# Graph attention and a mixture of experts on one core: where the normed row is added, which engines finish a tile, and the order of the opening loads

## Chip, cores, metric

One core of one Trainium2 chip runs the whole program in one launch. The metric is the device time of an execution in microseconds, the median of several runs of the same kernel.

## What is computed

There are 6250 nodes with 256 features and 206,250 edges, sorted by destination. Two layers follow each other. Shapes and names are cut to what matters:

```
h  = layernorm(x)                                  # (6250, 256)
z  = h @ W[head];  es = z.a_src;  ed = z.a_dst      # 4 heads of 64
e  = leaky_relu(es[src] + ed[dst], 0.01)
p  = exp(e - max over the edges of a destination)
x1 = x + (sum of p * z[src] over the edges) / (sum of p)

n      = layernorm(x1)                             # the "normed row"
logits = n @ gate_w + gate_b                       # 16 experts, the best 2 of each node
s0, s1 = softmax(top 2 logits)                     # s0 + s1 = 1
f_k    = relu(n @ w1[e_k] + b1[e_k]) @ w2[e_k] + b2[e_k]
y      = n + s0 * f_0 + s1 * f_1
out    = x1 + layernorm(y) * gamma + beta
```

Since s0 + s1 = 1, y is also s0 * (n + f_0) + s1 * (n + f_1).

## The kernel before, in words

The nodes lie in 49 tiles of 128 (`NT`; the last has 106 rows). The program has five stages, each ended by a barrier of all engines. Every engine has its own instruction stream. The helper `pipeline` (L50) writes such a stream out: for each round `i` it calls each listed function for item `i - lag`, in the order of the list, with a peeled head, a hardware loop and a tail. So the order within an engine is fixed by hand, and only semaphores tie the engines together.

- **Opening stage** (from L231). The SyncE queue (SP) loads `W`, then x in four parts of 12 tiles (`XC` = 4, `PART` = 12, L237), then the 106-row rest. It then waits for each part and passes the news on to VectorE (DVE) as `a_arrived` (L243), and after that stores the 49 projected tiles to `z_table` (L247). The ScalarE (ACT) queue loads the edge lists `src_raw` and `dst_raw` (L266 to L270) and gate_b, gamma and beta (L273). DVE forms the attention columns of `wcat` (L331, L332), the statistics of the first 12 tiles (L337), the inverse deviations (L171 to L176, L342), and then norms a tile (L355) for each that TensorE (PE) transposes (L456) and projects (L464). ACT copies both results from PSUM (L289, L297) into a ring of four `z_out`. GpSimd (POOL) sets `acc`, the sums of all tiles, to zero in one memset (L317).
- **Edge stage** (from L471). DVE first finds the largest and smallest source score; POOL takes the maximum over partitions (L541); from it comes `npass`, which every engine reads. Then 451 visits follow: POOL gathers rows of `z_table` by indirect DMA (L552), and PE, DVE and ACT weigh and sum them. This is the long stage, and the change leaves its loop alone.
- **Routing stage**. The new x1, its norm (kept in DRAM as `norm_rows`), the gate, and the lists of which node goes to which slot of which expert.
- **Expert stage** (L1093 on). Some 108 tiles of 128 slots. For a tile j, POOL fetches its normed rows by indirect DMA into `rows_sb` (`fetch`, L1140), PE transposes them (L1161), DVE copies the transpose (`copy_xT`, L1227), ACT copies `w1` (`copy_w1`, L1194) and then issues the load of the bias row `b2` of the expert, repeated on 128 partitions, into slot j mod 4 of `b2_sb` (L1198; the profile calls it `b_sb`). PE computes both products (L1171, L1183) with a relu on ACT between them (L1206). DVE adds the bias row (`add_b2`, L1232) and POOL stores the tile to `pair_rows` (`put`, L1147). Two orders matter for the change. On ACT, round j holds `copy_w1(j)`, the bias load of j and `relu(j-2)`; the load waits until `add_b2(j-4)` is done, as that frees the slot. On DVE, round i holds `copy_src(i)`, `copy_xT(i-3)`, `copy_dst(i-6)`, `add_b2(i-6)`.
- **Final stage** (L1242 on), 49 tiles, ring of 8. SP loads the two expert rows of each node and the normed row (L1316, L1317). ACT multiplies the first by s0 (L1262), POOL adds the normed row (L1270), DVE adds s1 times the second (L1279), takes the statistics (L1284, L1289), the inverse (L1293, the root is on ACT, L1257), subtracts the mean and multiplies by gamma (L1297), and multiplies by the inverse deviation and adds x1 + beta (L1303). SP stores the tile (L1324).

Of the kernel before, what the change touches and what calls it, by code (L numbers as in the profile page):

```python
# [33 lines left out]
RMAX = bass.bass_isa.ReduceOp.max  # L34
# [14 lines left out]
AHEAD = 6  # L49
ROWS = 4  # L50
# [41 lines left out]
def gnn_moe_kernel(nc, x, src, dst, W, a_src, a_dst, gate_w, gate_b, w1, b1, w2, b2, gamma, beta, out):  # L92
# [31 lines left out]
    def sem(name):  # L124
        return nc.alloc_semaphore(name=name)
# [10 lines left out]
    with whole:  # L136
# [27 lines left out]
        group_free = sb(graph, "group_free", [1, GROUPS], I32)  # L164

# [29 lines left out]
        a_x = [sem(f"a_x{i}") for i in range(XC + 1)]  # L195
        a_edges = sem("a_edges"); a_w = sem("a_w"); a_rows = sem("a_rows"); a_late = sem("a_late"); a_last = sem("a_last")
        a_vstep = sem("a_vstep"); a_bulk = sem("a_bulk"); a_arrived = sem("a_arrived"); 
        a_zeroed = sem("a_zeroed"); a_es = sem("a_es")
# [3 lines left out]
        a_xn = sem("a_xn"); a_xT_ps = sem("a_xT_ps"); a_xT = sem("a_xT"); a_z_ps = sem("a_z_ps")  # L202
        a_mod = sem("a_mod"); a_mod_saved = sem("a_mod_saved")
        a_z = sem("a_z"); a_store = [sem(f"a_store{i}") for i in range(4)]
        with ExitStack() as ctx:
# [13 lines left out]
            thr = sb(ctx, "thr", [P, 4])  # L219
            xn = sb(ctx, "xn", [P, 4, D])  # L220
            xnT = sb(ctx, "xnT", [P, 2, D])
            z_out = sb(ctx, "z_out", [P, 4, D + 2 * HEADS])
# [9 lines left out]
            def _(sp):  # L232
# [15 lines left out]
                pipeline(sp, NT, 4, 0, [(store, 0)])  # L248
                sp.wait_ge(a_mod, 1)
                sp.dma_start(dst_rows.rearrange("(b p f) -> p b f", p=P, f=P), dst_mod_h[:, :, :]).then_inc(a_mod_saved, 16)  # L250
                for s in range(4):
                    sp.wait_ge(a_store[s], 16 * len(range(s, NT, 4)))
# [3 lines left out]
            def _(act):  # L256
# [6 lines left out]
                act.wait_ge(a_padded, 3)  # L263
                tail = BLOCKS - 1
                for raw, e in ((src_raw, src), (dst_raw, dst)):
                    act.dma_start(raw[:, 0:tail, :], e[0:tail * P * P].rearrange("(b p f) -> p b f", p=P, f=P)).then_inc(a_edges, 16)  # L266
                    n = FULL_CHUNKS - tail * P
                    act.dma_start(raw[0:n, tail, :], e[tail * P * P:FULL_CHUNKS * P].rearrange("(p f) -> p f", f=P)).then_inc(a_edges, 16)
                    if E > FULL_CHUNKS * P:
                        act.dma_start(raw[n:n + 1, tail, 0:E - FULL_CHUNKS * P],  # L270
                                      e[FULL_CHUNKS * P:E].unsqueeze(0)).then_inc(a_edges, 16)
                for to, r in ((rows_bc[:, 2 * D:], gate_b), (affine[:, 0:D], gamma), (affine[:, D:2 * D], beta)):
                    act.dma_start(to, over(r.unsqueeze(0), [P, to.shape[-1]])).then_inc(a_late, 16)  # L273
# [17 lines left out]
                def copy_z(t, s, r):  # L291
                    act.wait_ge(a_z_ps, t + 1)
                    if not early(t, 4):
                        at, use = s % 4, r * (PART // 4) + s // 4
                        act.wait_ge(a_store[at], 16 * use)
                        act.wait_ge(a_es, t - 3)
                    nc.scalar.copy(z_out[:, s % 4, :], psZ[s % 2][:, 0:D + 2 * HEADS]).then_inc(a_z, 1)  # L297
                pipeline(act, NT, PART, PART, [(next_root, 0), (copy_xT, 0), (copy_z, 1)], tail=PART + 1)

            @block.gpsimd  # L300
            def _(pool):
# [11 lines left out]

                pool.wait_ge(a_edges, 16 * (6 if E > FULL_CHUNKS * P else 4))
# [1035 lines left out]
```

## Time and profile before

| | |
|---|---|
| median of 3 runs | 2931.32 us (2925.68 to 2935.93) |
| the profiled execution | 2933.89 us, of which the span of the trace is 2932.2 us |
| mean granted TensorE clock | 0.802 of full |
| busy: PE, DVE, ACT, POOL | 2224.2, 1807.8, 649.5, 1877.4 us |

How to read it: the profile gives for each engine the busy time, for each instruction its line, its start and duration, and for each stretch of idle time before one what ended it. PEld is the weight load of TensorE, which overlaps its products. A row with `ACTq` or `SPq` is a DMA issue on that queue; "to landing" counts from the start of the issue to the moment the transfer is seen. Line numbers in the rows are those of the kernel before; those of the changed kernel run up to 41 higher. A busy share of an engine is an average over five stages with different limits, so the stages are read one by one.

### The profile page before, as it was taken

To read this page: it belongs to the slowest core of one execution; us is meant where nothing else is said; L and a number is where in the kernel's file an instruction comes from. 1 tells how busy PE (TensorE), PEld (TensorE's weight loads), DVE (VectorE), ACT (ScalarE), POOL (GpSimd) and SP (SyncE) were. 2 spreads that over 40 slices of the span, in tenths; PEclk is the share of its full clock that TensorE was granted. 3 is DMA by queue.
4 is the path that set the end of the run, shared out by engine and by line. 5 is a ranking of instruction groups with operands and counts; after the bars stand their busy time and mean duration, and the time that the engine had idled before them with its cause. 6 is when DMAs were issued, how large, how long until landed. Compare 5 with 4: busy or idle time off the path is not lost. (4 is left out here: it accounts for less than half of the span.)

```text
span 2932.2 us, 63657 instructions
## 1 busy us (share of the span) xinstructions
PE 2224.2 (76%) x10753; PEld 1880.8 (64%) x10754; DVE 1807.8 (62%) x4852; ACT 649.5 (22%) x2612; POOL 1877.4 (64%) x1912
## 2 busy tenths in 40 slices
PE   3588778888778878778788788888855578999920
PEld 2477666676667766666666667667645358989920
DVE  6666666666666666666666666666668742222258
ACT  1311111111111111111111111111111234555532
POOL 2277777777777777777777777777753244545533
PEclk9877887877887778887887887787875589999965
DMA  4255555555555555555555555555541056333356
GB/s 147 88 142 137 135 134 136 135 135 135 135 134 135 136 133 136 138 135 134 135 136 135 134 135 137 134 134 135 137 134 63 25 189 186 104 100 106 104 165 206
DMA packets 298513, 386.43 MB, mean 132 GB/s; under 512 B 104451, under 2 KB 235883, under 8 KB 298475
## 3 DMA queue, kind: packets, MB, share of 16 engines
q0 software_dynamic: 87744, 243.02, 31.9%
q10 hardware_dynamic: 84912, 75.49, 10.5%
q1 hardware_dynamic: 125818, 67.52, 8.2%
q14 instruction: 28, 0.22, 0.0%
q8 instruction: 11, 0.18, 0.0%
HBM read 351.08 MB, written 33.93 MB: 131 GB/s over the span
## 5 line engine op out<-in xcount | busy, mean ns | idle before, releaser
L552 POOL DMA_INDIRECT ring<-z_table,idx_ring x1612 | 1552.1, 963 | 495.5 <-issue 452.2
L738 PE MATMUL psMb<-msg,xs 128*128 128x260 f32 x3608 | 1203.1, 491 | 259.9 <-DVE msg L649 258.2
L738 PEld LDWEIGHTS psMb<-msg,xs 128*128 128x128 f32 x3608 | 828.0, 241 | 433.8 <-issue 267.0
L727 PEld LDWEIGHTS psEb<-nodes,xs 128*128 128x128 f32 x3608 | 562.0, 227 | 260.2 <-issue 226.1
L727 PE MATMUL psEb<-nodes,xs 128*128 x3608 | 528.0, 274 | 156.6 <-DVE xs L607 153.8
L649 DVE TENSOR_TENSOR msg<-ring,psPb 128x1024 f32<-128x1024 f32 x451 | 545.7, 1210 | 0.0
L621 DVE TENSOR_TENSOR earg<-es_edge,psEb 128x16 f32<-128x16 f32 x451 | 76.5, 170 | 609.2 <-ACT es_edge L699 602.7
L699 ACT COPY es_edge<-ring 128x16 f32 x451 | 91.9, 204 | 1494.8 <-SPq L523 1321.9
L613 DVE TENSOR_TENSOR xs<-iota_f,psPb 128x512 f32<-128x512 f32 x451 | 306.2, 679 | 1.4 <-ACT psPb L708 0.2
L607 DVE TENSOR_SCALAR xs<-dst_bc,iota_p 128x512 f32<-128x512 bf16 x451 | 231.1, 513 | 39.9 <-issue 21.0
L1227 DVE COPY xT<-psXd 128x256 f32<-128x256 f32 x108 | 45.8, 424 | 317.6 <-PE psXd L1161 317.6
L1147 POOL DMA_INDIRECT pair_rows<-y_sb,dst_sb x108 | 107.6, 996 | 192.3 <-DVE src_sb L1216 124.2
L1171 PE MATMUL psHd<-xT,w_sb 128*128 128x128 f32 x1728 | 217.5, 281 | 0.0
L663 DVE TENSOR_TENSOR acc<-acc,psMb 128x260 f32 x451 | 188.6, 418 | 34.2 <-PE psMb L738 31.9
L1171 PEld LDWEIGHTS psHd<-xT,w_sb 128*128 128x128 f32 x1728 | 207.6, 197 | 0.6 <-issue 0.4
L1183 PE MATMUL psYd<-w_all,hid 128*128 x864 | 206.1, 382 | 0.0
L689 ACT ACTIVATE psPb<-dst_col,visit_base 128x4 f32 x451 | 120.6, 267 | 225.6 <-issue 179.2
L1183 PEld LDWEIGHTS psYd<-w_all,hid 128*128 128x128 f32 x864 | 157.8, 193 | 17.2
L1194 ACT COPY w_sb<-w_all 128x1024 f32 x108 | 112.8, 1045 | 185.4 <-PE psHd L1171 151.9
L1140 POOL DMA_INDIRECT rows_sb<-norm_rows,src_sb x108 | 106.6, 987 | 46.8 <-issue 32.9
L1206 ACT ACTIVATE hid<-psHd,b1T 128x128 f32<-128x128 f32 x432 | 123.1, 368 | 28.7 <-issue 24.5
L1270 POOL TENSOR_TENSOR got<-got 128x256 f32<-128x256 f32 x49 | 43.7, 892 | 74.5 <-ACT got L1262 74.5
(204 smaller groups left out, 1445.9 us busy)
## 6 DMA issues: line engine op xcount, KB each, us to landing
dst_bc<-dst_rows ACTq DMA_DIRECT2D x451, 128.0 KB
ring<-z_table,idx_ring POOLq DMA_INDIRECT x1612
w_all<-in_L_ffn_w_dram SPq DMA_DIRECT2D x32, 512.0 KB, 5.4
b_sb<-in_L_ffn_b_dram ACTq DMA_DIRECT2D x108, 128.0 KB, 3.0
got<-pair_rows SPq DMA_DIRECT2D x48, 256.0 KB, 2.9
xs<-in_x_dram SPq DMA_DIRECT2D x6, 1536.0 KB, 13.9
idx_ring<-src_idx SPq DMA_DIRECT2D x403, 2.0 KB
z_table<-z_out SPq DMA_DIRECT2D x49, 130.0 KB, 1.8
```

Source lines behind the costliest of these rows:

```text
L552: nc.gpsimd.indirect_dma_start(ring[:, s, c, :], None, z_table, bass.IndirectOffsetOnAxis(ap=idx_ring[:, s, c:c + 1], axis=0)).then_inc(b_ ...
L607: nc.vector.tensor_scalar(ST[:, s, :], dst_bc[:, at, :], iota_p[:, 0:1], None, ALU.is_equal).then_inc(b_ST, 1)
L613: nc.vector.tensor_tensor(S[:, s, :, :], over(iota_f[:, 0:P].unsqueeze(1), [P, G, P]), over(psP[s % 2][:, G * HEADS:G * HEADS + G].unsquee ...
L649: nc.vector.tensor_tensor(msg[:, s, :, 0:D].rearrange("p g (h d) -> p g h d", h=HEADS), ring[:, bass.ds(slot, 1), :, 0:D].rearrange("p o g ...
L663: nc.vector.tensor_tensor(at, at, psM[s % 2][:, 0:ROW], ALU.add).then_inc(b_acc, 1)
L689: nc.scalar.activation(psP[s % 2][:, G * HEADS:G * HEADS + G], dst_col[:, bass.ds(group * G, G)], ACT.Identity, bias=visit_base[:, bass.ds ...
L727: last = nc.tensor.matmul(dest_of(s)[:, c * SH:(c + 1) * SH], ST[:, s, c * P:(c + 1) * P], nodes[:, bass.ds(tile, 1), :].rearrange("p o c ...
L738: last = nc.tensor.matmul(psM[s % 2][:, 0:ROW], S[:, s, c, :], msg[:, s, c, :], start=c == 0, stop=c == G - 1)
L1171: last = nc.tensor.matmul(psH[s % 2][:, f * P:(f + 1) * P], w1_sb[:, s % 2, c, f * P:(f + 1) * P], xT[:, s % 2, c, :], start=c == 0, stop= ...
L1183: last = nc.tensor.matmul(psY[s % 2][:, 0:D], hid[:, s % 2, f, :], w2_f, start=f == 0, stop=f == FC - 1)
L1194: nc.scalar.copy(w1_sb[:, s % 2, :, :].rearrange("p c f -> p (c f)"), w_all[:, bass.ds(e, 1), 0:KD * F].rearrange("p o f -> p (o f)")).the ...
L1206: last = nc.scalar.activation(hid[:, s % 2, f, :], psH[s % 2][:, f * P:(f + 1) * P], ACT.Relu, bias=b1T[:, bass.ds(e, 1), f:f + 1].rearran ...
```

## The change

**Expert stage.** A new DVE step `add_row` (lag 3, right behind `copy_xT`) adds the normed rows `rows_sb` onto the bias row in `b2_sb`. It waits for the bias row to land. `add_b2` then waits for `add_row`, and so does `fetch`, before it overwrites `rows_sb`.

**Final stage.** The load of the normed row is gone. ACT makes a diagonal matrix of s0 and POOL one of s1; TensorE multiplies the two loaded rows by them and sums them in PSUM. DVE takes statistics and does the first scaling from PSUM; the second scaling goes to ACT (`to_unit`), the last addition to POOL (`finish`).

**Opening stage.** The first 12 tiles of x come in three loads of 4 (`a_piece`), and SP waits for these before it issues the rest. The edge lists and gate_b, gamma, beta move from the ACT queue to the SP queue, ahead of the stores of z. `acc` is set to zero tile by tile on ACT. The ring `z_out` grows from 4 to 6. POOL passes `a_arrived` on.

**Between opening and edge stage.** `npass` is found at the end of the opening stage, with the maximum over partitions taken by a transpose and a product on TensorE.

```
@@ opening stage, SP
-                for i in range(XC):
+                for i, landed in enumerate(a_piece):
+                    sp.dma_start(xs[:, i * PIECE:(i + 1) * PIECE, :],
+                                 x[i * PIECE * P:(i + 1) * PIECE * P]...).then_inc(landed, 16)
+                for landed in a_piece:
+                    sp.wait_ge(landed, 16)
+                for i in range(1, XC):
                     sp.dma_start(xs[:, i * PART:(i + 1) * PART, :], ...).then_inc(a_x[i], 16)
                 sp.wait_ge(a_padded, 1)
                 sp.dma_start(xs[0:REST, NT - 1, :], x[(NT - 1) * P:N]).then_inc(a_x[XC], 16)
-                for i in range(XC + 1):
-                    sp.wait_ge(a_x[i], 16)
-                    sp.nop().then_inc(a_arrived, 1)
+                sp.wait_ge(a_padded, 3)
+                for raw, e in ((src_raw, src), (dst_raw, dst)):
+                    sp.dma_start(raw[:, 0:tail, :], ...).then_inc(a_edges, 16)
...
+                for to, r in ((rows_bc[:, 2 * D:], gate_b), (affine[:, 0:D], gamma), (affine[:, D:2 * D], beta)):
+                    sp.dma_start(to, ...).then_inc(a_late, 16)
@@ opening stage, ACT (the same loads removed)
+                def zero_sums(t, s, r):
+                    if not isinstance(t, int) or t < NT - PART:
+                        at = bass.ds(t + PART, 1)
+                        nc.scalar.activation(acc[:, at, :]..., over(ones[:, 0:1], [P, ROW]), ACT.Copy, scale=0.0)
+                act.wait_ge(a_const, 5)
+                for t in range(PART):
+                    zero_sums(t - PART, 0, 0)
...
-                pipeline(act, NT, PART, PART, [(next_root, 0), (copy_xT, 0), (copy_z, 1)], tail=PART + 1)
+                pipeline(act, NT, PART, PART, [(next_root, 0), (copy_xT, 0), (copy_z, 1), (zero_sums, 0)], tail=PART + 1)
@@ opening stage, POOL
+                for i in range(XC + 1):
+                    pool.wait_ge(a_x[i], 16)
+                    pool.sem_inc(a_arrived, 1)
...
-                nc.gpsimd.memset(acc[:, :, :], 0.0).then_inc(a_zeroed, 1)
-                pool.wait_ge(a_zeroed, 1)
@@ opening stage, DVE
-                dve.wait_ge(a_arrived, 1)
                 for t in range(PART):
+                    if t % PIECE == 0:
+                        dve.wait_ge(a_piece[t // PIECE], 16)
                     tile_stats(t, 0, 0)
@@ edge stage, POOL
-                pool.wait_ge(b_spread, 1)
-                nc.gpsimd.partition_all_reduce(spread_all[:, :], spread[:, 0:SH], P, RMAX).then_inc(b_all, 1)
-                pool.wait_ge(b_passes, 1)
@@ expert stage, POOL
                     if not early(j, DR):
                         pool.wait_ge(d_xT_ps, j - DR + 1)
+                        pool.wait_ge(d_base, j - DR + 1)
@@ expert stage, DVE
+                def add_row(j, s, r):
+                    dve.wait_ge(d_b2[s], 16 * (r + 1))
+                    dve.wait_ge(d_xT_ps, j + 1)
+                    nc.vector.tensor_tensor(b2_sb[:, s, :], b2_sb[:, s, :], rows_sb[:, s, :], ALU.add).then_inc(d_base, 1)
+
                 def add_b2(j, s, r):
-                    dve.wait_ge(d_b2[s], 16 * (r + 1))
+                    dve.wait_ge(d_base, j + 1)
                     dve.wait_ge(d_down, j + 1)
...
-                pipeline(dve, None, DR, HEAD, [(copy_src, 0), (copy_xT, 3), (copy_dst, 6), (add_b2, 6), (add_beta, 0)], rounds=load_rounds(dve))
+                pipeline(dve, None, DR, HEAD, [(copy_src, 0), (copy_xT, 3), (add_row, 3), (copy_dst, 6), (add_b2, 6), (add_beta, 0)], rounds=load_rounds(dve))
@@ final stage, ACT
-                pipeline(act, NT, ER, ER, [(scale_first, 0), (root, 3)])
+                def spread_shares(t, s, r):
+                    if not early(t, 2):
+                        act.wait_ge(e_ps, t - 1)
+                    nc.scalar.activation(diag[:, s % 2, 0, :], ident[:, :], ACT.Copy, scale=share[:, 0, bass.ds(t, 1)]).then_inc(e_diag, 1)
+                def to_unit(t, s, r):
+                    act.wait_ge(e_fin, 2 * t + 2)
+                    nc.scalar.activation(y[:, s, :], y[:, s, :], ACT.Copy, scale=mv[:, s, 9:10]).then_inc(e_unit, 1)
+                pipeline(act, NT, ER, ER, [(spread_shares, 0), (root, 3), (to_unit, 4)])
@@ final stage, PE
+                    for k in range(TOP):
+                        last = nc.tensor.matmul(psS[s % 4][:, 0:D], diag[:, s % 2, k, :], got[:, s, k, :], start=k == 0, stop=k == TOP - 1)
@@ final stage, DVE
-                pipeline(dve, NT, ER, ER, [(add_second, 0), (variance, 1), (invert, 2), (scale, 2), (tile_stats, 0), (finish, 2)])
+                pipeline(dve, NT, ER, ER, [(tile_stats, 0), (variance, 1), (invert, 2), (scale, 2)])
@@ final stage, POOL
+                    nc.gpsimd.tensor_tensor(diag[:, s % 2, 1, :], ident[:, :], over(share[:, 1, bass.ds(t, 1)], [P, P]), ALU.mult).then_inc(e_diag2, 1)
...
+                    nc.gpsimd.tensor_tensor(y[:, s, :], y[:, s, :], xs[:, bass.ds(t, 1), :]..., ALU.add).then_inc(e_y, 1)
+                pipeline(pool, NT, ER, ER, [(spread_second, 0), (finish, 4)])
@@ final stage, SP
-                    sp.dma_start(got[0:n, s, TOP, :], norm_rows[bass.ds(t * P, n), :]).then_inc(e_got[s], 16)
```

How the instructions lie now, at the places where it matters. **VectorE in the expert stage's loop**, one round before (`ISA` rows are waits or register work; `d_b20` is the landing of a bias row in slot 0):

```order
L1216 COPY src_sb<-slot_ends 128x1
L1227 COPY xT<-psXd 128x256 [waits d_up,d_xT_ps]
L1221 ISA [waits d_stored0]
L1221 COPY dst_sb<-slot_ends 128x1
L1232 TENSOR_TENSOR y_sb<-psYd,b_sb 128x256 [waits d_down,d_b20]
```

and one round now:

```order
L1239 COPY src_sb<-slot_ends 128x1
L1250 COPY xT<-psXd 128x256 [waits d_up,d_xT_ps]
L1255 TENSOR_TENSOR b_sb<-b_sb,rows_sb 128x256 [waits d_xT_ps,d_b23]
L1243 ISA
L1244 ISA [waits d_stored0]
L1244 COPY dst_sb<-slot_ends 128x1
L1260 TENSOR_TENSOR y_sb<-psYd,b_sb 128x256 [waits d_down,d_base]
```

The wait for a landing has moved from the bias of the tile that is finished (three tiles older) to the bias of the tile whose transpose was just copied, and it now stands ahead of the addition that ends the older tile.

**The SP queue in the opening stage**, before:

```order
L234 DMA wcat<-in_L_gnn_W_dram 128x4x64 x2
L237 DMA xs<-in_x_dram 128x12x256 x4
L240 DMA xs<-in_x_dram 106x256 [waits a_padded]
L71 UNCONDITIONAL_BRANCH [waits a_x0,a_x1,a_x2,a_x3,a_x4]
L71 ISA
L247 ISA [waits a_z]
L247 DMA z_table<-z_out 128x260
```

and now:

```order
L242 DMA wcat<-in_L_gnn_W_dram 128x4x64 x2
L245 DMA xs<-in_x_dram 128x4x256 x3
L250 DMA xs<-in_x_dram 128x12x256 [waits a_piece2,a_piece1,a_x0]
L250 DMA xs<-in_x_dram 128x12x256 x2
L253 DMA xs<-in_x_dram 106x256 [waits a_padded]
L257 DMA src_raw<-in_src_dram 128x12x128 [waits a_padded]
L259 DMA src_raw<-in_src_dram 75x128
L261 DMA src_raw<-in_src_dram 1x42
L257 DMA dst_raw<-in_dst_dram 128x12x128
L259 DMA dst_raw<-in_dst_dram 75x128
L261 DMA dst_raw<-in_dst_dram 1x42
```

The loads of the edge lists (and behind them three small ones) now stand between x and the first store of z.

## Rows read from the trace of the kernel before

**Rows 1.** Stages, then a late stretch: us, busy (count) per engine, PEclk, DMA share, GB/s
```profile
143.00:2184.00 2041.00, 1654.01 (x7216) 1376.38 (x7216) 1355.93 (x3608) 307.52 (x1805) 1539.72 (x1609) 0.80 0.55 134
...
2363.00:2816.00 453.00, 415.41 (x2808) 382.93 (x2808) 112.88 (x444) 235.99 (x540) 214.17 (x216) 0.96 0.43 131
2816.00:2932.00 116.00, 0.00 (x0) 0.00 (x0) 100.29 (x294) 36.54 (x99) 43.67 (x49) 0.50 0.73 221
...
2830.00:2912.00 82.00, 0.00 (x0) 0.00 (x0) 81.26 (x237) 28.11 (x78) 35.96 (x40) 0.50 0.84 252
```

**Rows 2.** Opening stage timeline (59.62: seventh z): start us, us, engine, line, operation [idle before <-releaser]
```profile
1.89 19.07 SPq L237 DMA_DIRECT2D xs<-in_x_dram  x4
...
3.79 7.46 ACTq L268 DMA_DIRECT2D src_raw<-in_src_dram  x1
...
13.16 0.42 DVE L332 TENSOR_REDUCE wcat<-wprod 128x4 f32<-128x256 f32 x1
...
24.38 4.01 DVE L337 BATCH_NORM_STATS2 stats_a<-xs 128x6 f32<-128x256 f32 x12 [10.80 <-SPq L243]
...
29.82 12.13 DVE L172 TENSOR_SCALAR mean<-mean 128x12 f32<-128x12 f32 x1
31.21 10.71 POOL L317 MEMSET acc<- 128x12740 f32 x1
...
43.42 0.41 DVE L355 TENSOR_SCALAR xn<-xs,mean,rstd 128x256 f32<-128x256 f32 x1
...
59.62 0.38 ACT L297 COPY z_out<-psZa 128x264 f32<-128x264 f32 x1 [0.46 <-PE psZa L464]
```

**Rows 3.** Timeline of the start of the edge stage
```profile
118.87 0.50 DVE L561 TENSOR_REDUCE spread<-esed 128x4 f32<-128x196 f32 x1 [4.85 <-PEq L471]
...
127.06 0.36 DVE L584 TENSOR_SCALAR decided<-acc 128x196 f32<-128x196 f32 x1 [1.12 <-issue]
```

**Rows 4.** Timeline of one tile of the expert stage, DVE and the ACT queue
```profile
2600.90 0.34 ACTq L1198 DMA_DIRECT2D b_sb<-in_L_ffn_b_dram  x1
...
2602.64 0.42 DVE L1227 COPY xT<-psXd 128x256 f32<-128x256 f32 x1 [2.78 <-PE psXd L1161]
2602.98 0.14 DVE L1221 COPY dst_sb<-slot_ends 128x1 int32 x1
2603.11 0.42 DVE L1232 TENSOR_TENSOR y_sb<-psYd,b_sb 128x256 f32<-128x256 f32 x1
...
2604.63 0.34 ACTq L1198 DMA_DIRECT2D b_sb<-in_L_ffn_b_dram  x1
```

**Rows 5.** The bias loads from 2363 to 2475 us: durations, first and last start, landing
```profile
L1198 ACTq DMA_DIRECT2D b_sb<-in_L_ffn_b_dram x24: 339/340/407, 2368.7 to 2473.9; - x24
...
DMA to landing us min/median/max: 3.2/4.6/6.1
```

**Rows 6.** The same from 2475 us to the stage's end
```profile
L1198 ACTq DMA_DIRECT2D b_sb<-in_L_ffn_b_dram x84: 339/339/345, 2477.7 to 2791.9; - x84
...
DMA to landing us min/median/max: 2.9/2.9/3.5
```

**Rows 7.** Groups of the final stage: shapes, count | busy us, mean ns | idle before
```profile
L1270 POOL TENSOR_TENSOR got<-got 128x256 f32<-128x256 f32 x49 | 43.7, 892 | 74.5 <-ACT got L1262 74.5
L1279 DVE SCALAR_TENSOR_TENSOR y<-got,share 128x256 f32<-128x256 f32 x49 | 38.9, 794 | 19.5 <-POOL got L1270 18.8 <-issue 0.2
...
L1303 DVE SCALAR_TENSOR_TENSOR y<-y,mv,xs 128x256 f32<-128x256 f32 x49 | 23.6, 482 | 0.1
```

**Rows 8.** Timelines: a projected tile early and late in the opening stage, and the last load
```profile
49.27 1.97 PE L464 MATMUL psZa<-wcat,xnT 128*128 128x264 f32 x4
...
110.34 1.06 PE L464 MATMUL psZa<-wcat,xnT 128*128 128x264 f32 x4
...
2912.06 0.67 SPq L1317 DMA_DIRECT2D got<-norm_rows  x1
...
2921.81 0.51 ACT L1262 ACTIVATE got<-got,share 128x256 f32<-128x256 f32 x1 [5.20 <-DMA got<-norm_rows]
```

More of the change, by code:

```diff
@@ L33 @@
 AX = mybir.AxisListType
-RMAX = bass.bass_isa.ReduceOp.max
 P = 128
@@ L49 @@
 AHEAD = 6
+ZR = 6
 ROWS = 4
@@ L262, in _ @@
                                   .rearrange("g o -> o g")).then_inc(a_last, 16)
[L263 to L273, printed above, removed]
+                def zero_sums(t, s, r):
+                    if not isinstance(t, int) or t < NT - PART:
+                        at = bass.ds(t + PART, 1)
+                        nc.scalar.activation(acc[:, at, :].rearrange("p o c -> p (o c)"), over(ones[:, 0:1], [P, ROW]), ACT.Copy, scale=0.0)
+                act.wait_ge(a_const, 5)
+                for t in range(PART):
+                    zero_sums(t - PART, 0, 0)
                 def root(part, at):
@@ L292, in copy_z @@
                     act.wait_ge(a_z_ps, t + 1)
-                    if not early(t, 4):
-                        at, use = s % 4, r * (PART // 4) + s // 4
+                    if not early(t, ZR):
+                        at, use = s % ZR, r * (PART // ZR) + s // ZR
                         act.wait_ge(a_store[at], 16 * use)
-                        act.wait_ge(a_es, t - 3)
-                    nc.scalar.copy(z_out[:, s % 4, :], psZ[s % 2][:, 0:D + 2 * HEADS]).then_inc(a_z, 1)
-                pipeline(act, NT, PART, PART, [(next_root, 0), (copy_xT, 0), (copy_z, 1)], tail=PART + 1)
+                        act.wait_ge(a_es, t - ZR + 1)
+                    nc.scalar.copy(z_out[:, s % ZR, :], psZ[s % 2][:, 0:D + 2 * HEADS]).then_inc(a_z, 1)
+                pipeline(act, NT, PART, PART, [(next_root, 0), (copy_xT, 0), (copy_z, 1), (zero_sums, 0)], tail=PART + 1)
             @block.gpsimd
@@ L467, in _ @@
                 pipeline(pe, NT, 4, PART, [(aside, 0), (transpose, 0), (project, 1)], tail=PART + 1)
+                SH = 2 * HEADS
+                pe.wait_ge(a_edge_sb, len(EB))
+                pe.wait_ge(a_spread, 1)
+                nc.tensor.transpose(psA[3][0:SH, 0:P], spread[:, 0:SH], ident[:, :]).then_inc(a_spread_ps, 1)
+                pe.wait_ge(a_peak, 1)
+                nc.tensor.matmul(psA[3][:, P:P + SH], ones[0:SH, :], peak[:, 1:1 + SH], start=True, stop=True).then_inc(a_spread_ps, 1)
         nc.clear_and_free_semaphores(nc.allocated_since(before_a))
@@ new lines, in to_unit, with _, combine @@
+                def to_unit(t, s, r):
+                    act.wait_ge(e_fin, 2 * t + 2)
+                    nc.scalar.activation(y[:, s, :], y[:, s, :], ACT.Copy, scale=mv[:, s, 9:10]).then_inc(e_unit, 1)
+                pipeline(act, NT, ER, ER, [(spread_shares, 0), (root, 3), (to_unit, 4)])
+            @block.tensor
+            def _(pe):
+                def combine(t, s, r):
+                    pe.wait_ge(e_diag, t + 1)
+                    pe.wait_ge(e_diag2, t + 1)
+                    pe.wait_ge(e_got[s], 16 * (r + 1))
+                    if not early(t, 4):
+                        pe.wait_ge(e_fin, 2 * (t - 4) + 2)
+                    for k in range(TOP):
+                        last = nc.tensor.matmul(psS[s % 4][:, 0:D], diag[:, s % 2, k, :], got[:, s, k, :], start=k == 0, stop=k == TOP - 1)
+                    last.then_inc(e_ps, 1)
+                pipeline(pe, NT, ER, ER, [(combine, 0)])
@@ L1273, in _ @@
             @block.vector
             def _(dve):
[L1275 to L1280 removed]
                 def tile_stats(t, s, r):
[L1283 to L1284 removed]
+                    dve.wait_ge(e_ps, t + 1)
```

116 lines of the change are left out of this document (61 added, 55 removed).

## The prediction

> **What bounds the kernel now.** I read first the busy times of each stage, as the five stages have five limits. In the edge stage, 2041 us of the 2932, every engine but ACT is busy two thirds of the time or more; the change leaves that loop alone, so it is carried over unchanged [rows 1]. Of the expert stage's 453 us TensorE is busy 415, at 0.96 of its clock: it is the bound there, and DVE is busy for only 113. In the final stage DVE is busy 81.3 us of an 82 us stretch in which POOL does 40 tiles, so it is the bound at 2.1 us a tile, with the DMA engines 0.84 busy right behind it; TensorE does nothing [rows 1]. Next the timeline of the opening [rows 2]: nothing is normed before 43.42 us. DVE is done with `wcat` at 13.6, then waits for SP, which is busy issuing all of x until 21, before it hears at 24.38 that the first part has landed; then one tiny operation (L172) lasts 12.13 us, ending with the memset of `acc` on POOL. Last, 8.2 us pass at the start of the edge stage from the first reduction to the first operation that needs `npass` [rows 3].
>
> **Part 1, opening stage.** The SP issues run at about 4.8 us per 1.5 MB part (19.07 / 4) [rows 2], so the three pieces, one part in all, are issued by about 7 us and have landed by 11 or 12. The 12 statistics then start when `wcat` is done, at 13.6 instead of 24.38 (-10.8), and take the same 4 us. L172 no longer stands beside a memset: it should fall from 12.13 to the 0.17 or so of an operation on 12 elements like the rest, -12. Norming starts near 43.42 - 10.8 - 12 = 20.6. From there the pace is as before if nothing is late. Two things may be. Only now does SP issue the other 3 parts (14.5 us, till about 26), the rest and, new on this queue, the edge lists. One of those issues lasted 7.46 us on ACT, against traffic of x [rows 2]; alone I give each list 4 (an eighth of that again at the end for the small loads), so SP is free for the first store of z near 36. `z_out` has 6 slots, so the copy of the seventh z needs the first store landed, near 38. Before, the seventh z was copied at 59.62, 16.2 us after the first norm [rows 2]; by that pace it would be due at 37. DVE waits at its tenth tile for the edge lists, also about then. So the queue costs a us or so of a lead of 23. If each list keeps its 7.46 us, SP is free at 44, and the lead is 14; if nothing bites, it is 24. **-22, ends -14 and -24.** The 49 small zeroings on ACT (12 ahead of the loop, 37 in it, each like L297's 0.38 [rows 2]) lie beside the 1.06 us and more that TensorE needs a tile [rows 8]: three such ACT operations are 1.14 end to end, and less where they overlap. If that cover is thin, 37 of them cost up to 0.1 each, inside the room down to -14.
>
> [...]
>
> **Part 2, `npass`.** Its 13 small steps now run while the last stores land. From 118.87 to 127.06 is 8.2 us [rows 3]; a register load (1.12, the idle time before L584) and the copy of `nodes` stay: **-6.5, ends -5 and -8** (the lower if the added steps outlast the stores by 1 to 2 us).
>
> **Part 3, expert stage: one more DVE operation a tile, and a new loop.** The operation itself (0.42, by its like L1232 [rows 4]) is nothing to DVE at 113 of 453 us. Its wait is not. The bias row of tile j is issued at 2600.90 and takes 2.9 to land, so until 2603.8; the transpose of j is copied at 2602.64. Now `add_row(j)` stands there and waits, and queued behind it on DVE is `add_b2(j-3)`, for which ACT's bias load of j+1 waits (slot free), and behind that load on ACT stands `relu(j-1)`. So each load waits for the landing of the one before it: a chain that goes round once a tile. Its length: landing 2.9 [rows 6], `add_row` 0.34 (start to next start, as 2602.64 to 2602.98), 0.13 to the start of `add_b2`, 0.42 for it [rows 4], and about 0.15 until ACT issues: 3.95 us. The tile's pace now is 4.63 - 0.90 = 3.73 [rows 4]. The loop is longer by 0.22, and it binds after a few tiles, when TensorE's small lead is used up: 84 loads x 0.22 = 18.5. While the weights load (24 loads until 2475), a landing takes 4.6 in the middle [rows 5] and the loop 5.65, against a pace now of 105.2 / 23 = 4.6, in which there are already waits that it overlaps. At worst 24 tiles would each lose 1.07, some 25; I take half, 11. Less 4 us for hiccups that the slack then hides. **+25.** Ends: 0, if the landing is seen sooner than I think and all stays in TensorE's shade; +50, if the loop is 4.1 (0.37 x 84 = 31) and the early part is at its worst (20).
>
> [...]
>
> **Part 4, final stage.** DVE loses L1279 and L1303, 62.5 of its 100.3 busy us [rows 1, 7]; 37.8 stay, 0.77 a tile. The new limits per tile: DMA 384 KB for 512: 0.84 x 2.1 x 0.75 = 1.3 us at full use. POOL: one addition, 0.89 at most [rows 7], and a half-size product, together about 1.35. ACT: a root and a full-size scaling as before, 28.1 us in 39 tiles or 0.72 [rows 1], and a half-size one, about 0.35: 1.1. TensorE: a projected tile of 264 columns, the same number of passes, takes 1.06 at full and 1.97 at half clock [rows 8], so 1.03 and 1.91 here. It starts at half, as it has stood idle since the last expert tile (granted clock 0.50 [rows 1]). And the ring of waits from `combine` over statistics, scaling, `to_unit`, `finish` to the diagonal five tiles on goes round in about 4.4 us for three tiles, 1.45. I take 1.45. The stage: first load 3, four tiles at 1.91 = 7.6, 44 at 1.45 = 63.8, 2 of waiting for the last load (it took 9.7 us from 2912.06 [rows 8], and now carries two thirds), and the 10.4 from 2921.81 to the end of the span: 87 against 116 [rows 1]. **-30** with rounding. Ends: -38 (1.3 a tile), -16 (1.75).
>
> [...]
>
> **The sum:** -22 - 6.5 + 25 - 30 = -33.5. Against the profiled execution, 2933.9, that gives 2900.4; its time lies 2.6 above the median of 2931.3, so the forecast is **2898 us**. All ends together would be -70 and +15; they are not to be expected at once.
>
> **Rivals.**
> - *The added row is free* (chance 0.15). For it: TensorE has a lead of a few us, and the fastest landings may be seen earlier. Against: DVE's order and ACT's wait leave no way round. Then -58.5 alone: **2873**.
> - *The final stage does not speed up as thought* (0.15): TensorE stays at its half clock, the one granted all through the final stage now [rows 1], or the DMA engines hold at 2 us a tile. For it: TensorE would be idle a third of the time at full clock. Against: in the expert stage it keeps 0.96 of its clock [rows 1]. At 1.91 a tile, 44 x 0.46 = 20 of the 30 are lost: **2918**.
> - *The bias landing is long all the way* (0.10): the other side. Landings reach 3.5 in the quiet part [rows 6] and 4.6 while weights load [rows 5]. At 3.5 the loop is 4.55: 0.82 x 84 = 69 and 21 early, 90 in all against the 58.5 won: **2963**. It decides from the point where the quiet landings pass about 3.3: (58.5 - 11) / 84 = 0.57 over 3.73, so a loop of 4.3.
> - *SP is late in the opening* (0.08): lists at 7.46 us each and ACT crowded by zeroing: only 10 to 14 won, **2908**.
>
> The forecast has 0.52. A measurement of this kernel tells 0.3%, 9 us, from no change. The range 2866 to 2922 holds the forecast with its ends, the free row, the slow final stage and late SP, and leaves the long landing and half of the mixed bad cases out. Faster by over 0.3% (under 2922.5): 0.52 x 0.95 + 0.15 + 0.15 x 0.65 + 0.08 x 0.9 = 0.81; slower by over 0.3%: 0.09; within: 0.10.
>
> **What would show it.** Right: the first norm near 20 us; the stretch between stages 6 us shorter; in the expert stage a pace near 3.95, with idle time before L1255 ended by the bias DMA, and before TensorE's L1183 or ACT's relu; a final stage near 87 us with TensorE, POOL and the DMA engines all over two thirds busy. Wrong: an expert pace of 3.73 (step 3), a first norm after 30 us or z stored after 45 (step 1), or 1.9 us a tile with a clock of 0.5 in the final stage (step 4).

## The result and the profile after

The changed kernel takes **2924.9 us** (median of 20 runs, 2919.57 to 2930.41), against 2930.63 for the kernel before in 20 runs: a ratio of 0.998, 95% interval 0.9972 to 0.9988. Of the 33.5 us that the sum promised, 5.7 came in the medians. The profiled execution took 2920.8 us with a span of 2919.1, and it is the one the stages are read from; it lies 4.1 under its median, and that of before 3.3 over its own, so the two profiles differ by 13.1 us where the medians differ by 5.7.

The stages by their first instructions, in us (row ends are starts on the SP queue or on VectorE, as in the kernel before):

| stretch | before | after | difference | forecast |
|---|---|---|---|---|
| start to the first operation that needs `npass` | 127.1 | 100.9 | -26.1 | -28.5 |
| from there to the end of the edge stage | 2057.8 | 2071.5 | **+13.7** | 0 |
| routing | 178.3 | 174.6 | -3.7 | 0 |
| expert stage | 452.7 | 483.9 | +31.2 | +25 |
| final stage | 116.3 | 88.1 | -28.2 | -30 |
| span | 2932.2 | 2919.1 | -13.1 | -33.5 |

The same windows of the changed kernel as in [rows 1] (us, busy and count of PE, PEld, DVE, ACT and POOL, PEclk, DMA share, GB/s): edge loop, expert stage, final stage, and a stretch late in the final stage.

```profile
101.00:2172.00 2071.00, 1659.83 (x7216) 1380.59 (x7216) 1372.88 (x3618) 307.37 (x1805) 1566.46 (x1612) 0.79 0.54 133
2347.00:2831.00 484.00, 430.58 (x2808) 376.32 (x2808) 156.47 (x552) 236.32 (x541) 214.32 (x216) 0.97 0.40 123
2831.00:2919.00 88.00, 57.23 (x196) 36.42 (x196) 46.42 (x196) 55.94 (x148) 52.84 (x98) 0.89 0.71 219
2845.00:2909.00 64.00, 45.96 (x163) 28.49 (x161) 38.99 (x165) 46.56 (x125) 45.42 (x84) 0.97 0.83 254
```

The last line holds 163 products, four a tile, so 40.75 tiles in 64 us: 1.57 a tile. The DMA engines are as busy there as they were in the late stretch before (share 0.83 and 254 GB/s, against 0.84 and 252 [rows 1]), with three quarters of the bytes a tile (384 KB for 512).

**Opening.** Timeline of the changed kernel, the counterpart of [rows 2] (start, us, engine, line, operation, idle time before it and what ended that):

```profile
13.60 4.02 DVE L357 BATCH_NORM_STATS2 stats_a<-xs 128x6 f32<-128x256 f32 x12
17.87 0.17 DVE L174 TENSOR_SCALAR mean<-mean 128x12 f32<-128x12 f32 x1
19.51 0.41 DVE L376 TENSOR_SCALAR xn<-xs,mean,rstd 128x256 f32<-128x256 f32 x1
...
26.26 4.47 SPq L259 DMA_DIRECT2D src_raw<-in_src_dram  x1
...
31.64 2.42 SPq L259 DMA_DIRECT2D dst_raw<-in_dst_dram  x1
...
36.07 8.79 SPq L269 DMA_DIRECT2D z_table<-z_out  x9
...
40.06 0.38 ACT L316 COPY z_out<-psZa 128x264 f32<-128x264 f32 x1 [3.99 <-issue]
...
94.52 0.50 DVE L447 TENSOR_REDUCE spread<-esed 128x4 f32<-128x196 f32 x1
...
100.94 0.36 DVE L608 TENSOR_SCALAR decided<-acc 128x196 f32<-128x196 f32 x1 [1.11 <-issue]
```

The statistics start when `wcat` is done, the 12 us operation (L172 before, L174 now) takes 0.17, and norming begins at 19.51. SP reaches its first store at 36.07, and the seventh copy of z waits 3.99 us for it.

**Edge loop.** The gathers of POOL between 150 and 2150 us (durations min/median/max in ns), first before, then after:

```profile
L552 POOL DMA_INDIRECT ring<-z_table,idx_ring x1585: 942/946/1203, 149.9 to 2149.0; - x199
```

```profile
L586 POOL DMA_INDIRECT ring<-z_table,idx_ring x1575: 950/957/1221, 149.3 to 2149.3; - x197
```

Not a line of this loop was changed, yet the shortest gather is 8 ns longer and the median 11. Over all 1612 the groups on the page give 1552.1 us before and, after:

```profile
L586 POOL DMA_INDIRECT ring<-z_table,idx_ring x1612 | 1566.5, 972 | 552.6 <-issue 451.2
```

That is 14.4 us more, against the 13.7 of the table. Before nearly every gather stands a gap of 0.3 us and nothing else (before 1445 of the 1575 above, 440.2 us in all; 39.6 us went to waits for VectorE), so on this chip POOL's gathers set the pace of the stage and every nanosecond of one counts 1612 times.

**Expert stage.** One tile of the changed kernel, as [rows 4]; then its quiet bias loads, as [rows 6]:

```profile
2600.37 0.34 ACTq L1221 DMA_DIRECT2D b_sb<-in_L_ffn_b_dram  x1
...
2601.86 0.42 DVE L1250 COPY xT<-psXd 128x256 f32<-128x256 f32 x1 [1.55 <-PE psXd L1184]
...
2603.39 0.43 DVE L1255 TENSOR_TENSOR b_sb<-b_sb,rows_sb 128x256 f32<-128x256 f32 x1 [1.10 <-DMA b_sb<-in_L_ffn_b_dram]
...
2603.81 0.42 DVE L1260 TENSOR_TENSOR y_sb<-psYd,b_sb 128x256 f32<-128x256 f32 x1
...
2604.40 0.34 ACTq L1221 DMA_DIRECT2D b_sb<-in_L_ffn_b_dram  x1
```

```profile
L1221 ACTq DMA_DIRECT2D b_sb<-in_L_ffn_b_dram x85: 339/339/345, 2463.1 to 2806.6; - x85
...
DMA to landing us min/median/max: 2.9/3.0/3.5
```

The loop foreseen is there to be read: issue 2600.37, landing and `add_row` 3.02 later, `add_b2` 0.42 later, the next issue 0.59 later, 4.03 in all. Over the 84 intervals the mean is 4.09, against 314.2 / 83 = 3.79 before [rows 6].

### The profile page after: what moved, and what is told of

It reads as the page before. It is cut to its first block and busy times, and to the rows that moved or that the text cites. A ratio compares the mean times of both kernels' runs of the same rounds, so it can differ in the third digit from the quotient of the medians.

```text
span 2919.1 us, 64443 instructions
## 1 busy us (share of the span) xinstructions
PE 2304.5 (79%) x10952; PEld 1917.1 (66%) x10953; DVE 1786.3 (61%) x4864; ACT 684.8 (23%) x2711; POOL 1896.2 (65%) x1959
## 5 line engine op out<-in xcount | busy, mean ns | idle before, releaser
L760 PEld LDWEIGHTS psMb<-msg,xs 128*128 128x128 f32 x3608 | 837.2, 243 | 439.0 <-issue 267.5
L1255 DVE TENSOR_TENSOR b_sb<-b_sb,rows_sb 128x256 f32<-128x256 f32 x108 | 45.9, 425 | 148.0 <-DMA b_sb<-in_L_ffn_b_dram 148.0
```

The source lines that it names most:

```text
L760: last = nc.tensor.matmul(psM[s % 2][:, 0:ROW], S[:, s, c, :], msg[:, s, c, :], start=c == 0, stop=c == G - 1)
```

## Experiments

Fourteen runs in four sets. Ratios are to the kernel before on the same chip.

| kernel | median us | of before | 95% interval |
|---|---|---|---|
| row_after_b2 | 2885.82 | 0.9851 | 0.9822 to 0.9880 |
| opening_only | 2910.10 | 0.9942 | 0.9923 to 0.9962 |
| npass_only | 2929.06 | 1.0005 | 0.9992 to 1.0018 |
| expert_final_only | 2931.72 | 1.0024 | 1.0011 to 1.0036 |
| reduce_kept_again | 2878.87 | 0.9813 | 0.9793 to 0.9833 |
| reduce_then_iota_again | 2876.07 | 0.9815 | 0.9795 to 0.9836 |
| two_more_posts | 2888.82 | 0.9856 | 0.9836 to 0.9875 |
| four_more_posts | 2890.39 | 0.9865 | 0.9844 to 0.9887 |
| load_only | 2879.39 | 0.9818 | 0.9796 to 0.9839 |
| load_zero_again | 2889.57 | 0.9857 | 0.9836 to 0.9878 |

The second set (reduce_kept, reduce_then_iota, three_rows_on_pe, lists_on_act) ran on a chip on which the edge stage of every kernel took some 950 us longer (before: 3887.69 us), so only its other stages and the length of its gathers are used. Its ratios were 0.9836, 0.9852, 0.9880 and 0.9830 in that order. There POOL's gathers did not set the pace: its waits for VectorE between 150 and 2150 us came to 671 to 687 us, against 39 to 45 in the other sets, and the two kernels with the longer gathers had the shorter edge stage (3003.3 and 3001.8 us, against 3013.2 and 3010.4).

### The parts one by one

Each is the kernel before with one part of the change put in, and nothing else.

> The kernel before with the opening part of the change alone (pieces, lists on SP, zeroing on ACT, six z slots). Both theories: z is done 20 to 24 us sooner. Theory A (the longer gathers of the edge stage, median 957 ns in the changed kernel against 946, come with the removal of the partition-wide maximum on POOL or with nothing in this part): gathers stay at 946, the total is 22 to 24 us below before. Rival B (the longer gathers come with this part): gathers at 957, edge stage 12 to 15 us longer, total only 8 to 12 below before.

> The kernel before with npass alone moved (found at the end of the opening stage, maximum over partitions on TensorE, no partition_all_reduce on POOL). Theory A (POOL's gathers are longer after a program that never ran partition_all_reduce): gathers at 957 ns, edge stage 12 to 15 us longer, total 7 to 12 above before. Rival B (they have nothing to do with it): gathers at 946, total 2 to 6 below before.

> The kernel before with the expert and the final part of the change. Expert stage +28 to +32, final stage -27 to -30 by the ledger of the two profiles, so the total is within 4 us of before. Gathers: at 946 ns if their length comes with the opening or the npass part; at 957 if it is none of the parts but the placement of the program or the chip.

The parts add up: -0.58%, +0.05% and +0.24% make -0.29%, against -0.20% measured for all of them, which is the same within their intervals. The opening brings `npass`'s first user forward by 19.4 us (127.06 to 107.69), with gathers at 946 ns: its theory A for the gathers. The total fell by 16 us (interval 11 to 23) where 22 to 24 were expected; between the two traces it is 23.9. The expert and final parts cancel, +27.8 and -28.8 us, again at 946 ns; the total was expected within 4 us of before and came out 7 above (interval 3 to 11), 4.1 below between the traces. The `npass` part saves 7.2 us ahead of the edge loop (127.06 to 119.91) and then gives it back there: its edge stage is 2066.1 us against 2057.8. That is theory A in kind and short of it in size: 8.3 us longer and not 12 to 15, 953 ns and not 957, and a total that did not move instead of rising by 7 to 12. Its gathers:

```profile
L570 POOL DMA_INDIRECT ring<-z_table,idx_ring x1579: 949/953/1223, 149.2 to 2149.0; - x198
```

So the longer gathers come with the `npass` part. 953 is not quite the 957 of the whole change; the 4 ns between them stayed unexplained.

The maximum itself, last input to first use of the result, before and after:

```profile
119.94 0.17 DVE L563 TENSOR_SCALAR spread<-spread 128x4 f32<-128x4 f32 x1
...
124.51 0.39 POOL L541 PARTITION_ALL_REDUCE spread_all<-spread  x1 [82.58 <-issue]
125.01 0.17 DVE L567 COPY level<-spread_all 128x4 f32<-128x4 f32 x1 [4.69 <-POOL spread_all L541]
```

```profile
95.60 0.17 DVE L449 TENSOR_SCALAR spread<-spread 128x4 f32<-128x4 f32 x1
...
97.23 0.16 DVE L454 COPY level<-psA 128x4 f32<-128x4 f32 x1 [0.47 <-PE psA L510]
```

```profile
46.98 0.40 POOL L343 PARTITION_ALL_REDUCE spare<-ones  x1 [6.09 <-issue]
```

An iota of 0.13 us waited like that too, 6.94 us behind its own two records (reduce_then_iota_again, L344), while behind the pair at a program's start POOL is idle for 0.31 us at the most. So most of what the move to TensorE saved is that load. No run made the load earlier and kept the maximum on POOL, and none has the reduction without a load.

### The loop through the landing

```
-  [(copy_src, 0), (copy_xT, 3), (add_row, 3), (copy_dst, 6), (add_b2, 6), (add_beta, 0)]
+  [(copy_src, 0), (copy_xT, 3), (copy_dst, 6), (add_b2, 6), (add_row, 3), (add_beta, 0)]
```

> The changed kernel with one edit: in VectorE's round of the expert stage add_row(j) stands behind add_b2(j-3), not ahead of it. Theory A (the loop through the landing: bias load, landing 3.0 us, add_row, add_b2, next bias load, 4.03 us around): nothing of the loop is left, so the quiet pace falls from 4.03 to 4.09 us a tile back to 3.73 to 3.79, the expert stage from 484 to 455 to 460 us, and the total to about 2897 (2924.9 - 28). [...]

Theory A held, and by more than it asked: the stage is back at 452.3 us (452.7 before), the pace at (2779.3 - 2476.2) / 80 = 3.79, the total at 0.985 of before where the whole change had 0.998. The stage gives 31.6 us; the 38 between the two ratios have an interval of some 9. The same work is done, and the added operation itself is not what cost: it still runs 108 times, at 425 ns (L1255), with the pace back at 3.79. Only who stands behind the wait is different. Timeline of VectorE and of the ACT queue, and the loads from 2475 us:

```profile
2650.49 0.42 DVE L1260 TENSOR_TENSOR y_sb<-psYd,b_sb 128x256 f32<-128x256 f32 x1
2651.38 0.42 DVE L1255 TENSOR_TENSOR b_sb<-b_sb,rows_sb 128x256 f32<-128x256 f32 x1 [0.47 <-DMA b_sb<-in_L_ffn_b_dram]
```

```profile
2652.18 0.34 ACTq L1221 DMA_DIRECT2D b_sb<-in_L_ffn_b_dram  x1
```

```profile
L1221 ACTq DMA_DIRECT2D b_sb<-in_L_ffn_b_dram x81: 339/340/345, 2476.2 to 2779.3; - x81
```

VectorE still waits for the landing in nearly every round (0.47 us here, 36.7 us in 82 waits from 2470 us on, against 96.5 in 83), but `add_b2`, which frees the slot of the next load, is done before that wait begins, so the wait no longer holds up the next load.

### What makes a gather longer

```
+                nc.gpsimd.partition_all_reduce(spare[:, :], ones[:, 0:8], P, RMAX)        # reduce_kept
+                nc.gpsimd.iota(spare_i[:, :], [[1, 1]], base=0, channel_multiplier=1)     # reduce_then_iota, behind it
```

> row_after_b2 with one more edit: at the end of the opening stage POOL, otherwise idle there, runs one partition_all_reduce whose result nobody reads. [...] Theory A (the loaded library sets the length of a gather): median gather back from 957 to 946 ns, edge stage 12 to 15 us shorter than in row_after_b2, the total 9 to 13 us below it, as the load of library 0 in the routing stage (about 3 us) comes back. Rival B (the placement of the instructions, or another piece of the npass part): gathers stay at 957, total unchanged or up to 4 us longer.

> reduce_kept with one iota of 128 numbers behind the reduction, so that library 0 is loaded again ahead of the gathers. Theory A (the loaded library): gathers at 957 ns again and the time of row_after_b2. Rival B (it is enough that the reduction has run once, or that instructions are placed a little further on): gathers at 946 and the time of reduce_kept.

On the disturbed chip the medians were 949 and 946 ns. So the reduction brings the short gathers back, but my theory A fell: with library 0 loaded again (two records on the iota's L344, at 47.7 and 47.8 us, and none on the next, L845) they stay short. Two theories were left, that the reduction (with its load) has run, and the place of POOL's loop in its stream. The place was put to the test by itself, with two and four empty semaphore posts in place of the reduction:

```
+                for _ in range(2):          # four in four_more_posts
+                    pool.sem_inc(apart, 1)
```

> row_after_b2 with two empty semaphore posts of POOL at the end of the opening stage: POOL's loop of gathers then stands two instructions further on in its stream, and nothing else differs. Theory A (library or reduction: something that only the reduction brings): gathers at 957 ns, as in row_after_b2, and its time, 0.985 of before. Rival B (the place of POOL's loop in its instruction stream sets the length of a gather): gathers at 946 to 949 ns, edge stage 12 us or more shorter, total near 0.981 of before.

> The same with four empty posts: POOL's loop stands where it stands in reduce_then_iota. Theory A (the reduction): 957 ns. Rival B (the place): 946 ns, as in reduce_then_iota, edge stage 12 us or more shorter than in row_after_b2, total near 0.981 of before.

> reduce_kept once more, as the edge stage of its first chip was held up by something else for 950 us in every kernel. On a chip as the first: gathers 946 to 949 ns; if a gather's length is what the edge stage goes by (1612 gathers one behind the other on POOL), the edge stage is near 2058 us, against 2074 in row_after_b2, and the total near 0.981 of before. If it is not, the total is that of row_after_b2, 0.985.

> reduce_then_iota once more, for the same reason. Its gathers were at 946 ns there, so the library that is loaded is not what counts, and the two theories left are that the reduction has run, or the place of the loop in the stream. Gathers 946 ns, edge stage 12 us or more shorter than in row_after_b2, and a total near 0.981 of before.

The place is not it. Gathers of four_more_posts, then of reduce_then_iota_again, whose loop stands at the same place:

```profile
L588 POOL DMA_INDIRECT ring<-z_table,idx_ring x1572: 950/957/1220, 150.1 to 2149.7; - x197
```

```profile
L592 POOL DMA_INDIRECT ring<-z_table,idx_ring x1583: 942/949/1209, 149.9 to 2148.1; - x198
```

Edge stages: 2074.2 in row_after_b2, 2072.0 and 2075.0 with the posts, 2061.2 and 2059.6 with the reduction, and the totals follow (0.9856 and 0.9865 against 0.9813 and 0.9815). The last pair parts the reduction from its load. Its two kernels have one instruction each at the same place and differ ahead of the gathers only in which library it loads:

```
+                nc.gpsimd.load_library(library_config._reserved_1)    # load_only: library 1
+                nc.gpsimd.load_library(library_config.standard)       # load_zero_again: library 0, already there
```

> row_after_b2 with one POOL instruction more at the end of the opening stage, ahead of the gathers: the load of library 1 alone, without the reduction. Theory A (the load in mid-program is what makes the gathers shorter): gathers 946 to 949 ns, edge stage near 2060 us, total near 0.9815 of before. Rival B (the reduction itself does it, a load alone does not): gathers 957 ns, edge stage near 2074 us, total near 0.985.

> The same, but the instruction loads library 0, the one that is already there. Theory A1 (any load instruction does it): gathers 946 to 949 ns and the time of load_only. Theory A2 (only the exchange of the library does it): gathers 957 ns and the time of row_after_b2, 0.985 of before.

```profile
L588 POOL DMA_INDIRECT ring<-z_table,idx_ring x1582: 942/949/1227, 149.3 to 2149.1; - x198
```

```profile
L588 POOL DMA_INDIRECT ring<-z_table,idx_ring x1574: 950/957/1220, 149.4 to 2149.8; - x197
```

Settled by these, for this loop: what shortens the gathers is that another library than the iotas' has been loaded once before them, library 1 in load_only. The reduction is not needed (942/949 ns in load_only), the library need not still be there (942/949 in reduce_then_iota_again), and to load the one already loaded does nothing (950/957 in load_zero_again). The edge stages of the last pair are 2063.7 and 2071.9 us, its medians 2879.39 and 2889.57. Over all runs outside the second set the edge stage is 2053.9 to 2063.7 us with a load of another library than 0 ahead of it and 2066.1 to 2075.0 without. The fetch of rows in the expert stage shows it in its shortest only (942 to 949 ns with the load, 952 to 960 without, all sixteen traces), and not in its median (970 or 973 in both groups). Why POOL issues the same gather 8 ns faster afterwards no run here shows. The routing stage carries the other end: where a reload of library 0 stands in it (the pair of records on its iota's line), it takes 177.4 to 178.3 us (before, opening_only, expert_final_only, reduce_kept_again, load_only), and 174.6 to 175.9 in the others. So the -3.7 us of the routing stage is in the main that reload, gone with the reduction: the two groups lie 1.5 to 3.7 us apart.

### What the final stage's gain hangs on

```
+                    last = nc.tensor.matmul(psS[s % 4][:, 0:D], ident[:, :], got[:, s, TOP, :], start=False, stop=True)
+                    sp.dma_start(got[0:n, s, TOP, :], norm_rows[bass.ds(t * P, n), :]).then_inc(e_got[s], 16)
```

> The changed kernel without the expert part: the final stage loads the normed row again as a third row, and TensorE adds it by a third product with the identity. It asks what the final stage's gain of 28 us hangs on. Theory A (the load left out, as the DMA engines are near full there): 1.75 to 1.8 us a tile, the stage 99 to 102 us against 88 and 86, 12 to 16 slower than row_after_b2. Rival B (DVE was the bound, relieving it was all): the stage at 88 to 92 us, and the total within 5 us of row_after_b2. The expert stage should take 453 us in both.

The edit is made to the changed kernel with its expert part taken back. The stage took 106.2 us, 18 more than reduce_kept on the same chip (88.5), so theory A, beyond its range of 99 to 102; the expert stage took 452.0. The window of the stage, then its first two groups (count | busy, mean ns | idle before):

```profile
3731.00:3837.00 106.00, 77.49 (x294) 54.94 (x294) 46.44 (x196) 59.32 (x148) 53.25 (x98) 0.90 0.78 242
```

```profile
L1304 PE MATMUL psSe<-got,diag 128*128 128x256 f32 x196 | 57.4, 417 | 34.0 <-DMA got<-norm_rows 30.5 <-DVE mv L1322 1.3 <-POOL diag L1338 0.7
L1342 POOL TENSOR_TENSOR y<-y,xs 128x256 f32<-128x256 f32 x49 | 35.5, 725 | 38.3 <-ACT y L1292 38.3
```

VectorE has as little to do here as in the changed kernel (46.4 us), and yet the stage is only 10 us shorter than before. Of the 28 us, then, 10 come from relieving VectorE and 18 from leaving out the load: relieved of one bound, the stage ran at once into the other. Two limits of this reading: the third product is work for TensorE too, 30.6 us in all, though TensorE stood idle for 30.5 us waiting for the third row; and the other order, the load left out with VectorE's work kept, was not run. VectorE was busy 81.3 of 82 us before [rows 1], so it is likely, but not shown, that leaving out the load alone would have won little.

### The lists on SP or on ACT

The block of list loads was moved, unchanged, from behind SP's loads of x to ACT's queue, ahead of `zero_sums`.

> row_after_b2 with the edge lists and gate_b, gamma, beta issued from the ACT queue again, ahead of the zeroing of acc. It tests the step on SP's queue: in the changed kernel SP reaches the first store of z at 36.07 us, and the seventh z was copied at 40.06, after 4 us of waiting. Theory A (SP's list issues cost those us): SP is free near 24 us, no wait before the seventh z, z done 3 to 5 us sooner than at 94.3. Rival B (the lists collide with x on ACT's side, as in the kernel before, where one issue took 7.5 us, and hold up ACT's zeroing and first copies): z done at the same time or later, by up to 10 us.

```profile
15.86 8.80 SPq L250 DMA_DIRECT2D xs<-in_x_dram  x3
...
30.09 12.35 SPq L256 DMA_DIRECT2D z_table<-z_out  x7
```

And ACT:

```profile
17.14 1.28 ACT L289 ACT_TABLE_LOAD   x1 [16.98 <-issue]
18.43 3.81 ACT L289 ACTIVATE acc<-ones 128x260 f32<-128x260 f32 x12
22.25 1.28 ACT L296 ACT_TABLE_LOAD   x1
23.55 0.31 ACT L296 ACTIVATE rstd<-ln_tmp,eps_col 128x12 f32<-128x12 f32 x1
```

Rival B, in its mildest form: z was done 3.0 us later (97.98 against 94.94 in row_after_b2, and in three_rows_on_pe on the same chip). SP is free at 30.1 instead of 36.1 (24 was expected) and no copy of z waits for it, so the step on the queue was right. But ACT issues the lists from 3.2 to 14.8 us and the small loads until 17.1, and only then zeroes its 12 tiles, at 18.43; in the changed kernel it does so at 4.48. Behind the zeroing stands the root that the inverse deviations need, at 23.55 instead of 18.91, though VectorE had its input ready at 19.0. So the first transposed tile is copied at 25.41, not 20.77. That the lists travel beside the pieces of x moves SP's wait for the pieces from 13.98 to 15.86, but not the statistics, which start at 13.75 against 13.60. So it is issue time on both sides: SP won 6 us of it, and ACT lost it ahead of work that was waited for.

## Why the prediction was wrong

The forecast was 2898 us in 2866 to 2922, and "faster" 0.81; the median is 2924.9, 27 over the forecast and 3 over the range, and by less than 0.3% faster. By the steps, against the profiles (13.1 us won for 33.5, a miss of 20.4 us):

- **The edge stage "is carried over unchanged"** (+13.7, and -3.7 in routing; forecast 0). This is the step that failed, and with it the range, which had no term for it; the sum put the stage at nothing without a reason beyond the unchanged loop. What the runs showed in its place: without the library load that comes with the reduction each of the 1612 gathers of POOL takes 8 to 11 ns more, 14.4 us in all. "The change leaves that loop alone" was true of the code and not of the state in which POOL reaches it: Part 2 counted what the reduction cost where it stood, and not what its library load did for 1612 gathers afterwards. No row of the kernel before shows it; what could be seen there is that one nanosecond on a gather costs 1.6 us, so that a part which touches POOL's program deserved an end of its own.
- **Part 3, the expert stage** (+31.2, forecast +25, ends 0 and 50). The mechanism was right to each link, and row_after_b2 shows it by taking it away. Sizes: the loop was 4.03 and not 3.95, as it is 3.0 us from the issue until VectorE goes on, and not 2.9. The quiet part cost 84 x 0.30 = 25, forecast 14.5: 0.08 x 84 = 7 of that are the loop, and the 4 us credited for hiccups never came, since the mean pace stands 0.06 over the loop now as it did before. The early part cost (4.83 - 4.57) x 24 = 6 (106.3 us for 22 intervals from 2352.7 on, against 105.2 for 23), forecast 11; half was still too much.
- **Part 4, the final stage** (-28.2, forecast -30). 88.1 us against 87. The pace in the middle is 1.57 a tile and not 1.45; TensorE's longest wait in the stage is for `got`, 24.6 us. What the sum did not part is what the gain consists of: it went from VectorE's 2.1 us a tile to a ring of waits at 1.45, with the DMA engines at 1.3 and so out of the way; by three_rows_on_pe 18 of the 28 us hang on the load left out, and the DMA engines are as busy as before. The addition of `finish` takes 726 ns on POOL (L1347), 1.6 times the 466 of VectorE's scaling of the same shape (L1333). It cost nothing, as POOL is busy 45 of 64 us.
- **Part 1, the opening** (-19.4 alone, forecast -22). First norm at 19.51 (forecast 20.6), SP free at 36.07 (36), seventh z at 40.06 (38). The hold on the queue was named and was sized at "a us or so"; it is 4.
- **Part 2, `npass`** (-7.2 alone, forecast -6.5). Right in its place. The maximum itself fell from 4.9 us to 1.46, most of it the library load ahead of the reduction.

Where the maximum stood, TensorE was the faster way for it, by 3.4 us, but only as POOL had a library to load first: the reduction's own 0.39 us is less than the 1.46 of TensorE's way. Counting what the gathers gained by that load (8.3 us between npass_only and before, 14.4 between the whole change and before), the reduction on POOL came out ahead.

The rivals: the added row was not free, the final stage did not stay slow (granted clock 0.97 in its late stretch), the landings stayed at 3.0, and SP was in time. None was the case, and none had POOL's gathers in it.

## What to carry to other kernels

When a wait moves to another place in an engine's order, write down who stands behind it and whether that one's end starts the very thing waited for; if so, the latency has become the pace, and the cure may be to swap two entries of a list (here 31.6 us in the stage). Count how many times the bounding instruction runs, and take any edit to that engine's program, even outside the loop, as one that may shift its length (here it did, by a library load): compare the minimum and the median of that one instruction between two traces before anything else. When an engine is relieved, ask which of its two causes, work or data, the next bound is, and try them one at a time.

## What was not expected of the hardware

- A gather of the edge stage by indirect DMA took POOL 940 to 942 ns at the least and 946 to 949 in the median in every kernel that had loaded another library than that of its first iota at some time before (library 1 in load_only, the reduction's in seven), and 947 to 950 and 953 to 957 in every kernel that had not: sixteen traces, on at least three chips. Loading the library that is already there changes nothing (950 and 957, load_zero_again). In this program of 1612 gathers the edge stage is 8 to 15 us shorter with the load of another (2063.7 against 2071.9 in the last pair, 2059.6 against 2075.0 with the loop at the same place), as long as POOL sets the pace.
- POOL was idle for 6.09 us between its last cast and a reduction of 0.40 us, with the two records of the library load at the start of that time (reduce_kept_again), and for 6.94 us behind the next load, ahead of an iota of 0.13 us (reduce_then_iota_again).
- The versions with the swapped list entry and such a load ahead of the gathers (reduce_kept_again, reduce_then_iota_again, load_only: 0.9813 to 0.9818 of before) are level with each other, and by those ratios about 1.65% faster than the changed kernel (0.998), by an order in a list and an operation whose result nobody reads, or the bare load in its place.
